# Six local-attention layers on one core: one projection piece turned ahead of the next projection, two projections placed between another tile's turns

## The reference

```
for i in range(6):
    q, k, v = split(shift_tokens(x) @ Wqkv[i])            # 128 -> 3 * 1024
    q, k = l2norm(q) * q_scale, l2norm(k) * k_scale        # 16 heads of 64
    q, k = rotary(q), rotary(k)                            # cos, sin and a scale by position
    sim = 8 * q @ k.T       # a window of 32 tokens and the one before it
    out = softmax(where(mask, -max, sim)) @ v
    x = out @ Wo[i] + x
    x = ffn(layernorm(shift_tokens(x))) + x                # 2 * 341 hidden, gelu gate
```

## Time and profile before

| | us |
|---|---|
| median of 3 runs | 4533.77 (4532.44 to 4534.2) |
| the profiled execution, its own time | 4532.7 |
| its span in the profile | 4530.8 |
| TensorE busy | 4314.1 (95%) |
| VectorE busy | 3280.0 (72%) |
| ScalarE busy | 2751.0 (61%) |
| GpSimd busy | 2194.4 (48%) |

### The profile page before, as it was taken

One profiled execution on the slowest core, in us unless ns is written; L12 is line 12 of the kernel. 1 busy time (PEld: TensorE's weight loads), 2 busy tenths in 40 slices (PEclk: granted clock), 3 DMA queues, 4 the chain that ended last, 5 costly groups with the idle time before them and its releaser, 6 DMA issues. The chain is left out here.

```text
span 4530.8 us, 172607 instructions
## 1 busy us (share of the span) xinstructions
PE 4314.1 (95%) x68826; PEld 2566.0 (57%) x68826; DVE 3280.0 (72%) x5787; ACT 2751.0 (61%) x5465; POOL 2194.4 (48%) x1997
## 2 busy tenths in 40 slices
PE   7999999998699999999999999999999999999997
PEld 4555555555356555556556556556556555556554
DVE  4666666665477777877777777777777877777775
ACT  4545555454466666666666666666666666666664
POOL 0000000000366666666666666666666666666763
PEclk9999999999899999999999999999999999999998
DMA  1000000000121112111121111211122111221112
GB/s 39 8 6 8 8 6 6 8 6 4 42 59 49 45 48 67 52 46 49 48 68 50 46 47 50 70 46 49 47 60 59 47 45 49 63 53 49 49 43 80
DMA packets 145061, 189.72 MB, mean 42 GB/s; under 512 B 34151, under 2 KB 66298, under 8 KB 144250
## 3 DMA queue, kind: packets, MB, share of 16 engines
q1 hardware_dynamic: 144250, 178.39, 14.6%
HBM read 29.39 MB, written 4.19 MB: 7 GB/s over the span
## 5 line engine op out<-in xcount | busy, mean ns | idle before, releaser
L1395 POOL TENSOR_TENSOR cs<-cs 128x512 f32<-128x512 f32 x768 | 977.0, 1276 | 530.9 <-DVE cs L1729 527.5
L1522 PE MATMUL psum<-wqkv,xw 128*128 128x512 f32 x2304 | 1191.7, 609 | 35.9 <-DVE tiled L1670 26.3
L1729 DVE TENSOR_TENSOR cs<-psum,rots 128x1024 f32<-128x1024 f32 x768 | 933.9, 1221 | 230.9 <-PE psum L1522 220.0
L1404 POOL TENSOR_TENSOR qk<-cs,rn 128x512 f32<-128x512 f32 x768 | 776.6, 1043 | 330.7 <-ACT rn L1595 304.2
L1611 ACT ACTIVATE sq<-psum 128x512 f32<-128x512 f32 x768 | 458.8, 597 | 613.8 <-DVE cs L1729 584.9
L1430 POOL MEMSET qTl<- 128x2048 f32 x1 | 1.8, 1804 | 1169.9 <-POOLq L522 1169.9
L1683 DVE TENSOR_REDUCE ss<-sq 128x8 f32<-128x512 f32 x768 | 520.1, 677 | 6.9
L1466 PEld LDWEIGHTS psum<-pT,vw 64*64 64x64 f32 x18624 | 401.1, 135 | 186.7 <-issue 186.2
L1527 PEld LDWEIGHTS psum<-ident,qk 128*128 128x128 f32 x3088 | 356.8, 142 | 226.6 <-issue 164.3
L1522 PEld LDWEIGHTS psum<-wqkv,xw 128*128 128x128 f32 x2304 | 368.7, 190 | 200.1 <-issue 174.6
L1527 PE MATMUL psum<-ident,qk 128*128 128x128 f32 x3088 | 445.0, 278 | 21.3 <-POOL qk L1404 13.2
(11 more groups left out here) (205 smaller groups left out, 6744.9 us busy)
## 6 DMA issues: line engine op xcount, KB each, us to landing
vw<-vl SPq DMA_DIRECT2D x768, 128.0 KB, 2.4
vw<-vl SPq DMA_DIRECT2D x672, 64.0 KB, 2.0
wqkv<-in_wqkv SPq DMA_DIRECT2D x42, 256.0 KB, 4.0
wol<-in_wol SPq DMA_DIRECT2D x7, 512.0 KB, 4.0
w1l<-in_w1l SPq DMA_DIRECT2D x7, 341.0 KB
xin<-in_x SPq DMA_DIRECT2D x9, 256.0 KB, 2.8
xr<-in_x SPq DMA_DIRECT2D x8, 256.0 KB, 2.8
sums<-sumout SPq DMA_DIRECT2D x8, 256.0 KB, 2.3
```

The costliest lines, as they stand in the source:

```text
L1395: summed_rot.done(nc.gpsimd.tensor_tensor(own, own, halves(cs[:, t % 2, j, 1, :])[:, :, ::-1, :], ALU.add), at)
L1404: rotated.done(nc.gpsimd.tensor_tensor(qk[:, j, :].rearrange("p (h c) -> p h c", c=EL), cs[:, t % 2, j, 0, :].rearrange("p (h c) -> p h c" ...
L1522: last = nc.tensor.matmul(ps[:, :], xw[:, t * P:(t + 1) * P], wqkv[:, col:col + BANK], start=True, stop=True)
L1729: parts.done(V.tensor_tensor(cs[:, t % 2, j, :, :].rearrange("p i (h c) -> p i h c", c=EL), twice, by_head, ALU.mult), at)
```

## The change

Only the order of `BODY` is changed, and only in its first third. `t.3.3` comes ahead of `qk.0.2`. Behind `v.0.1`, `qk.1.1` comes ahead of all four turns of tile 0 where it stood ahead of the last, `qk.1.2` comes between the second and the third of them where it stood behind `oa.2`, and `qk.1.3` comes ahead of `o.2.0` where it stood behind `o.2.1`. `w.3` keeps its place among the steps in which VectorE and GpSimd have a part. No instruction is added or dropped.

```
@@ -188,9 +188,9 @@
 BODY = [step(name) for name in """
-    qk.0.0 t.3.0 qk.0.1 t.3.1 t.3.2 qk.0.2 t.3.3 qk.0.3 n.0 pt.2.0 qk.1.0 sa.3
-    v.0.0 pt.2.1 s.3.0 s.3.1 v.0.1 t.0.0 t.0.1 w.3 t.0.2 qk.1.1 t.0.3 oa.2
-    qk.1.2 o.2.0 o.2.1 qk.1.3 pt.3.0 sa.0 n.1 pt.3.1 v.1.0 s.0.0 s.0.1 qk.2.0
+    qk.0.0 t.3.0 qk.0.1 t.3.1 t.3.2 t.3.3 qk.0.2 qk.0.3 n.0 pt.2.0 qk.1.0 sa.3
+    v.0.0 pt.2.1 s.3.0 s.3.1 v.0.1 w.3 qk.1.1 t.0.0 t.0.1 qk.1.2 t.0.2 t.0.3 oa.2
+    qk.1.3 o.2.0 o.2.1 pt.3.0 sa.0 n.1 pt.3.1 v.1.0 s.0.0 s.0.1 qk.2.0
     v.1.1 t.1.0 w.0 t.1.1 oa.3 t.1.2 qk.2.1 o.3.0 o.3.1 t.1.3 qk.2.2 pt.0.0
```

## The result

The changed kernel takes 4583.93 us (median of 4 runs, 4579.98 to 4585.62) against 4533.99 for the kernel before on the same chip: 1.0109 times as long, 95% interval 1.0096 to 1.0121. That is 50 us more. The prediction was 24 us more, 4558, with a range up to 4580: the right direction, half the size, and outside the range.

What follows compares the result with a forecast made beforehand. TensorE, busy for 682.52 of 700 us, was taken to bound the kernel. Longer repeats, 31 us, less 7 us of issue gaps gave 24 on 4532.7, so 4557, plus 1.1 for the median: 4558, range 4538 to 4580.

Steps and rivals of the forecast that it cites:

- The removed waits: TensorE's waits at the masked scores of tile 3 and the turns of tile 0 go, 0.60 and 0.78 us.
- the new wait: Output of tile 2 waits 1.83 us a repeat for ScalarE's square of `qk.1.1`, which holds its bank.
- the common point: First turn of tile 3's probabilities, `pt.3.0`, beyond which both orders agree: reached at 1978.86 instead of 1978.34.
- The sum's first term: Repeats grow by 0.55 us in six of a layer's eight and 0.93 in the first two: 31 us.
- The wait that the second edit makes: Step deriving 1.83 us: eight back from `o.2.1` stands `qk.1.1`, whose square waits for VectorE's late product.
- The sum: 31 us of longer repeats less 7 us of shrinking issue gaps: 24 us more than before, 4558.
- (a): Issue gaps all go, 27 us off the 31: 4 us more than before, 4538; chance 0.10.
- (b): No wait at the output of tile 2, `pt.3.0` 1.31 us earlier: 63 us less, 4471; chance 0.07.
- (c): Issue gaps grow as tile 3's scores find instructions missing: 4572, or 4585 with half as many again; chance 0.11.

Runs made afterwards that it cites:

- e1: Kernel before with only `t.3.3` moved ahead of `qk.0.2`: 4533.46 us, 1.0005 times the kernel before.
- e3: Changed kernel with `w.3` two turns later, behind `t.0.1`, TensorE's order kept: 4503.77 us, 0.9938 times the kernel before.
- e5: Changed kernel with the first turn of tile 0 ahead of `qk.1.1`, moving the ring by one: 4512.63 us, 0.9953 times the kernel before.
- e4: Changed kernel with two unused projections computed in the wait ahead of the output of tile 2: 4566.54 us, 1.0080 times the kernel before.
- e6: Kernel of e3 with `v.1.0` ahead of the masked scores of tile 0: 4506.02 us, 0.9937 times the kernel before.
- e7: Kernel of e4 with one added projection instead of two: 4571.74 us, 1.0087 times the kernel before.
- e8: Kernel of e3 without the first edit, `t.3.3` behind `qk.0.2` as before: 4526.79 us, 0.9987 times the kernel before.
- e9: Kernel before in its own order, output of tile 2 made to wait for the square of `qk.1.1`: 4705.21 us, 1.0367 times the kernel before.
- e10: Kernel of e9 with the rest filled by two added projections: 4627.40 us, 1.0214 times the kernel before.

## Why the prediction was half the size

**The removed waits, the new wait and the common point** were right, as rows after and e1, e3 and e5 show: the bank of `qk.1.1` makes the wait (e5), VectorE's chain ahead of that product sets its end (e3), and the first edit alone is worth nothing (e1). Only the latency behind the square was 0.14 us instead of 0.24. The sum's first term, 31 us, was also met, but partly by luck. Without the low stretches a repeat grew by 0.67 us on the mean over the eight places in a layer, 31 us in all. Of this only 0.57 arose up to `pt.3.0`, 27 us: 0.4 in the third to the sixth repeat of a layer (forecast 0.55), 0.65 and 0.67 in the first two (forecast 0.93), but 0.93 and 0.74 in the last two, for which the forecast had 0.55. The other 4 us arose behind `pt.3.0`, where it had nothing. Why, no run tested; the issue gaps grew by 10 us in the layers.

**The step that failed is "The wait that the second edit makes"**: it was priced at its length, 1.83 us (1.54 in the record) less what it replaced, and at nothing else. What it set off was a second price, the clock. The forecast had no term for that at all, though the clock's column was on the page. That it was 1.00 before was no proof that it would stay: the layers before had six rests of 1.2 to 1.7 us, none with a low stretch behind it, where the new order has 48 of 1.5 to 1.7. The longest of the six:

```profile
2307.21 0.41 PE L1485 MATMUL psum<-maskw,tiled 64*32 64x512 bf16 x8 [1.68 <-ACT kTl L1624]
```

Set against repeats at the same place in a layer, the nine repeats with a low stretch are 21 us longer together. Taking the rest away at the same wait gave 15 to 17 us (e4), so the size is 15 to 21 us of the 26 that were missing.

The Trainium skill's page "TensorE: Matmul & The Clock Gate", section "A second HAM failure mode: psum-queue depth-cycling", tells of a kernel whose short idles between groups of matmuls, from cycling through the banks, make the clock go to and fro. This case agrees in that an idle of 1.5 us made by a bank was enough, in 9 repeats of 48. It would have been a rule to weigh, and it was not.

**"The sum"** had also 7 us for issue gaps that would shrink behind a long rest, and this term was wrong: they did not (4.9 us in eight repeats against 4.5). So 31 - 7 = 24 becomes 31 + 21 = 52, against 51.3 measured.

**The rivals.** (a) is out by the same rows. (b), no binding bank, is what e5 shows for another order: the wait goes, and the time is 19 us below before, not 63. Up to `pt.3.0` a repeat of e5 is 1.02 us shorter (forecast 1.31), but behind it 0.61 comes back: the mask waits for the copy of `t.0.3` (15.3 us over the layers), and the issue gaps are 41 us instead of 26. The sum of (b) stopped at `pt.3.0` and didn't look for what is late next. (c), growing gaps, came in part: the maximum of `s.3.0` was early as forecast, but the gaps grew by 10 us in the changed kernel, and again in e6.

**Open.** Why nine waits of 48 are followed by a low stretch and not the others, with rests that are alike, is not settled. Nor is it settled whether the place of a rest counts besides its length: in the layers of the twelve traces stand 78 other rests of 1.2 us and more, and only the two in e6 have a low stretch behind them. What ends the issue gaps, and why they grew in the changed kernel, e5 and e6, is open too.

## What to carry to other kernels

In a ring of buffers, moving a step changes whose reader each later step waits for: list the reader eight back for every step behind the edit, and ask which of them is late by its own engine's chain. A rest of the matrix engine costs its length and may cost the clock for several times as long behind it, so a rest that can't be removed is cheaper filled; half of it was enough here (e7). A wait ahead of another one is worth nothing alone and may be worth a lot once the other is gone (0 in e1, 23 us in e8), so pairs are to be tried together.

## What the runs showed of the hardware

A rest of TensorE of some 1.5 us once in 69 was enough for its clock to fall to the lower level in 9 of 48 repeats; a rest of 2.0 us did so 39 times (e9). All 59 low stretches in the layers of the twelve traces stand at a rest of 1.5 us or more; all but one begin up to 1.8 us behind its end, that one 0.2 us ahead of it (e9). Of the 78 rests of 1.2 to 1.8 us at other places two have one, both in e6. Each such stretch lasted 3.4 to 10.2 us and cost 2.3 us on the mean in the changed kernel and 2.5 in e9. Useless matmuls in the rest removed them all: TensorE did more and the kernel was 78 us faster (e9, e10).
